# Cross-attention and tree-routed FFN on one core: both layer norms scaled by ScalarE, the constant score rows copied by DMA, and batch 2's score parts made between the first scores

## What is computed

```python
def layernorm(x): return (x - mean(x)) / sqrt(var(x) + 1e-5)      # over the features
# part 1: causal attention of 16 heads of 16, weights scaled so that scores are large
xn = layernorm(x)
q, k, v = xn @ w_q.T, ctx @ w_k.T, ctx @ w_v.T                    # split into 16 heads
x = x + softmax(causal(q k^T / 4)) v @ w_o.T
# part 2: three trees (q, k, v) of depth 4 route each token to one of 16 leaf MLPs (256 -> 64 -> 256)
z = layernorm(x)
q, k, v = fff_q(z), fff_k(z), fff_v(z)
x = x + softmax(q k^T / 16) v
```

## Time and profile before

| what | value |
|---|---|
| median of 3 runs | 679.64 us (678.51 to 679.95) |
| the profiled execution | 676.23 us |
| its span, first to last instruction | 674.4 us |
| around the span | 1.8 us |
| mean granted TensorE clock | 0.948 |
| PE busy | 558.6 us (83%) |
| DVE busy | 488.7 us (72%) |
| POOL busy | 355.2 us (53%) |
| ACT busy | 307.1 us (46%) |

### The profile page before, as it was taken

How to read it: one execution, slowest core, us unless ns; L and a number is a source line. 1 busy time by engine, 2 the same in 40 slices (tenths; PEclk the granted TensorE clock), 3 DMA queues, 4 the chain that set the end, 5 groups by cost and what they waited for, 6 DMA issues and landing times.

```text
span 674.4 us, 15294 instructions
## 1 busy us (share of the span) xinstructions
PE 558.6 (83%) x5375; PEld 454.7 (67%) x5375; DVE 488.7 (72%) x1411; ACT 307.1 (46%) x508; POOL 355.2 (53%) x452
## 2 busy tenths in 40 slices
PE   7637899989899888989888775849998888679996
PEld 6525678756676666767666553738887777569995
DVE  3887678999999999999998874772555455046664
ACT  3201555544454454445444452006876766433231
POOL 6551444466675675666656558512105666565642
PEclk9967999999999999899999997878999999999999
DMA  6696578757867875786776149847999999756663
GB/s 185 188 294 182 192 241 249 215 182 243 263 193 238 258 214 197 236 235 195 227 233 206 56 145 303 249 142 265 357 361 400 343 386 337 247 154 195 188 190 124
DMA packets 105715, 156.98 MB, mean 233 GB/s; under 512 B 12362, under 2 KB 75946, under 8 KB 105642
## 3 DMA queue, kind: packets, MB, share of 16 engines
q1 hardware_dynamic: 93786, 129.45, 60.7%
q0 software_dynamic: 9216, 25.18, 11.7%
q10 hardware_dynamic: 2640, 1.40, 0.7%
HBM read 84.20 MB, written 71.30 MB: 231 GB/s over the span
## 4 chain that ended last, share of the span: by engine, by line
PE 41%; DVE 27%; issue 13%; POOL 8%; ACT 5%; DMA 4%; another core or an unknown queue 1%; DVEq 0%; SPq 0%; POOLq 0%; ACTq 0%
DVE mneg L1194 8%; PE banks L841 5%; PE banks L527 5%; DVE xn L1142 4%; PE banks L830 4%; PE banks L902 4%; PE banks L856 4%; POOL xs_dram L1584 3%; PE banks L923 3%; DMA xb<-xs_dram 3%; POOL pt L1596 2%; PE banks L694 2%; PE banks L561 2%; ACT pt L956 2%; PE banks L891 2%
## 5 line engine op out<-in xcount | busy, mean ns | idle before, releaser
L956 ACT ACTIVATE pt<-banks 128x768 f32<-128x768 f32 x128 | 103.5, 811 | 102.4 <-PE banks L562 76.9
L1596 POOL TENSOR_SCALAR_AFFINE_SELECT pt<-pt 128x512 f32<-128x512 f32 x128 | 81.9, 641 | 123.0 <-ACT pt L956 120.5
L1194 DVE TENSOR_REDUCE mneg<-banks 128x6 f32<-128x768 f32 x128 | 121.0, 948 | 15.1 <-PE banks L536 10.5
L1584 POOL DMA_INDIRECT xs_dram<-xn2s,place x96 | 95.9, 999 | 53.8 <-issue 16.4
L534 PE MATMUL banks<-k,q 96*128 96x128 bf16 x256 | 52.3, 227 | 52.6 <-DVE mneg L1194 51.7
L534 PEld LDWEIGHTS banks<-k,q 96*128 96x128 bf16 x256 | 25.5, 100 | 69.7 <-DVE mneg L1194 40.8
L577 PE MATMUL banks<-pt,vp 128*32 128x256 f32 (+1 forms) x1024 | 57.2, 343 | 9.3 <-issue 6.2
L561 PE MATMUL banks<-q,k 98*128 98x256 bf16 x256 | 57.0, 276 | 1.6
L1677 POOL DMA_INDIRECT q_all<-ys_dram,place x32 | 31.2, 976 | 45.9 <-DMA ys_dram<-yb 27.9
L535 PE MATMUL banks<-k,q 124*128 124x128 bf16 x256 | 51.9, 225 | 0.0
L536 PE MATMUL banks<-k,q 124*128 124x128 bf16 x256 | 51.6, 223 | 0.0
(11 more groups left out here) (182 smaller groups left out, 1426.9 us busy)
## 6 DMA issues: line engine op xcount, KB each, us to landing
ys_dram<-yb SPq DMA_DIRECT2D x36, 512.0 KB
xb<-xs_dram SPq DMA_DIRECT2D x35, 512.0 KB
xs_dram<-zero SPq DMA_DIRECT2D x45, 256.0 KB
xs_dram<-zero SPq DMA_DIRECT2D x18, 384.0 KB, 4.7
parts_dram<-kp SPq DMA_DIRECT2D x16, 384.0 KB
k<-parts_dram SPq DMA_DIRECT2D x32, 192.0 KB
parts_dram<-qp SPq DMA_DIRECT2D x16, 384.0 KB
q<-parts_dram SPq DMA_DIRECT2D x32, 192.0 KB
```

The costliest lines, as they stand in the source:

```text
L956: nc.scalar.activation(pt[:, 2 * p:2 * p + 2, 0:S + P], st_banks(b, p)[:, :, 0:S + P], ACT.Exp, scale=SC / QS).then_inc(exp_sb, 1)
L1194: nc.vector.tensor_reduce(mneg[b % 2][:, 2 * j:2 * j + 2, :], two[:, :, 0:S + P].rearrange("p e (i k) -> p e i k", k=P), axis=AX.X, op=ALU ...
L1584: gp.indirect_dma_start(xs_dram[tree], bass.IndirectOffsetOnAxis(ap=place[:, k:k + 1], axis=0), xn2s[m % RING][:, t, :], None).then_inc(sc ...
L1596: pool.affine_select(out=diag, in_=diag, compare_op=ALU.is_ge, fill=0.0, base=0, pattern=[[0, 2 * T], [1, P]], channel_multiplier=-1).then ...
```

## The change

Both norms are scaled by ACT, as an activation `Identity` with `scale` = rs and `bias` = -mean times rs. POOL makes that bias with two more instructions of 128x2 per norm, so `rstd1` and `rstd2` count by two. In the loop ACT has the second norm at j == 3, ahead of `weighed(b, 0)` and of the second part of q, and the first norm at j == 6, ahead of the copy of the values. `kw` and `qw` are half as wide, both are built at the start of POOL's list, and POOL's four casts are gone: SP copies the rows of buffer 0 to buffers 1 and 2, with four DMAs behind the unloading of batch 1 and ahead of `load_x(3)`. DVE's cast of `q4[0]` moves to just behind the first statistics. In the ramp, the second parts are made by ACT. The projections, transposes and parts of batch 2, and the norm of batch 3, stand between the first natural scores on PE and between their maxima on DVE.

```diff
+            def const_copy(z):                                              # SP
+                sp.wait_ge(const_rows[0], 2)
+                for full in (q4, k4):
+                    sp.dma_start(full[z][KS:P, :, :], full[0][KS:P, :, :]).then_inc(const_rows[z], 16)
...
                 unload(1, 1)
                 unload(1, 0)
+                for z in range(1, BUFS):
+                    const_copy(z)
                 load_x(3)
...
-                pe.wait_ge(c_in[2], 16)                                     # PE, ramp
-                pe.wait_ge(k1_sb, 1)
-                pe.wait_ge(kr_sb, 1)
-                project(W_BANKS[0], wk, lambda c: ct[2][:, c, :]).then_inc(k_ps, 1)
...
-                transpose_in(2)
-                pe.wait_ge(xnT_sb, 3)
-                pe.wait_ge(v_sb, 1)
-                project(G7, wq, lambda c: xnT[:, c * S:c * S + S]).then_inc(q_ps, 1)
                 for j in range(PAIRS):
                     first_scores(j)
-                    if j == 5:
+                    if j == 1:
+                        transpose_in(2)
+                    if j == 2:
+                        pe.wait_ge(xnT_sb, 3)
+                        pe.wait_ge(v_sb, 1)
+                        project(G7, wq, lambda c: xnT[:, c * S:c * S + S]).then_inc(q_ps, 1)
+                    if j == 4:
+                        pe.wait_ge(c_in[2], 16)
+                        pe.wait_ge(k1_sb, 1)
+                        pe.wait_ge(kr_sb, 1)
+                        project(W_BANKS[0], wk, lambda c: ct[2][:, c, :]).then_inc(k_ps, 1)
+                    if j == 6:
                         transpose_in(3)
...
+            def norm_out(b):                                                # ACT
+                act.wait_ge(rstd1, 2 * (b + 1))
+                ge(act, xnT_ps, b - 1)
+                for t in range(T):
+                    nc.scalar.activation(xn[b % 2][:, t, :], xt[b % 2][:, t, :], ACT.Identity, scale=rs1[:, t:t + 1],
+                                         bias=mr1[:, t:t + 1]).then_inc(xn_done, 1)
+            def norm2_out(b, u):
+                act.wait_ge(rstd2, 2 * (b + 1))
+                ge(act, xn2T_ps, b - 1)
+                if b >= RING:
+                    for r in range(TREES):
+                        scattered(act, r, b - RING)
+                for t in range(T):
+                    nc.scalar.activation(xn2s[b % RING][:, t, :], x1[u][:, t, :], ACT.Identity, scale=rs2[:, t:t + 1],
+                                         bias=mr2[:, t:t + 1]).then_inc(xn2_sb, 1)
...
+                    if j == 3 and has(b, -2):
+                        norm2_out(b - 2, u)
                     if j == 3 and has(b, -1):
                         weighed(b, 0)
...
+                    if j == 6 and has(b, LEAD + 1):
+                        norm_out(b + LEAD + 1)
                     if j == 6 and has(b, 1):
...
+                norm_out(0)                                                 # ACT, ramp, behind the cast of k4[0]
                 first_part(kp, K1, W_BANKS[0], k_ps, 0, k1_sb, 1.0)
...
+                copy_xnT(0)
+                second_part(kp, K2, k_rem, kr_sb, 0, k2_sb)
+                q_parts(0)
+                norm_out(1)
+                k_parts(1, W_BANKS[1])
+                copy_xnT(1)
+                q_parts(1)
                 act.wait_ge(consts, 2)
                 act.wait_ge(v_ps, 1)
...
+                norm_out(2)
+                copy_xnT(2)
+                q_parts(2)
+                k_parts(2, W_BANKS[0])
+                norm_out(3)
...
-                    if j == 2 and has(b, -2):                               # DVE, loop
...
-                            nc.vector.tensor_scalar(xn2s[(b - 2) % RING][:, t, :], x1[u][:, t, :], mv2[:, t, 0:1],
-                                                    rs2[:, t:t + 1], ALU.subtract, ALU.mult).then_inc(xn2_sb, 1)
                     if j == 5 and has(b, -1):
                         divide(b, 1)
-                    if j == 5 and has(b, LEAD + 1):
-                        norm_out(b + LEAD + 1, u)
...
                 norm_in(0, 0, 0)                                            # DVE, ramp
+                v.wait_ge(q_factor, WIDE + 1)
+                nc.vector.tensor_copy(q4[0][KS:P, :, :].rearrange("p h (i k) -> p (h i) k", k=P),
+                                      qf.unsqueeze(1).to_broadcast([P - KS, NH * T, P])).then_inc(const_rows[0], 1)
                 k_parts(0, W_BANKS[0])
-                norm_out(0, 0)
                 norm_in(1, 0, 1)
-                norm_out(1, 1)
                 q_parts(0)
                 k_parts(1, W_BANKS[1])
+                q_parts(1)
                 norm_in(2, 1, 0)
...
                 for j in range(PAIRS):
                     first_maxima(j)
-                    if j == 1:
-                        norm_out(3, 1)
+                    if j == 3:
+                        q_parts(2)
+                    if j == 4:
+                        norm_in(3, 1, 1)
+                    if j == 5:
+                        k_parts(2, W_BANKS[0])
                 last_maxima(0)
...
                 pool.tensor_scalar(ve[:], mv[:, :, 1], EPS, None, ALU.add).then_inc(var_sem, 1)   # POOL, rsqrt
-                gp.wait_ge(var_sem, b + 1)
+                pool.tensor_scalar(mr[:], mv[:, :, 0], -1.0, None, ALU.mult).then_inc(var_sem, 1)
+                gp.wait_ge(var_sem, 2 * (b + 1))
                 pool.tensor_tensor(rs[:], ve[:], mhalf[:], ALU.pow).then_inc(rstd_sem, 1)
+                gp.wait_ge(rstd_sem, 2 * b + 1)
+                pool.tensor_tensor(mr[:], mr[:], rs[:], ALU.mult).then_inc(rstd_sem, 1)
...
-                for z in range(1, BUFS):                                    # POOL, ramp
-                    pool.tensor_copy(k4[z][KS:P, :, :], kf.unsqueeze(1).to_broadcast([P - KS, NH, S])
-                                     ).then_inc(const_rows[z], 1)
-                    pool.tensor_copy(q4[z][KS:P, :, :], qf.unsqueeze(1).to_broadcast([P - KS, NH, S])
-                                     ).then_inc(const_rows[z], 1)
...
+                for m in range(2, LEAD + 1):
+                    rsqrt(m, aggr1, mv1, ve1, var1, rs1, mr1, rstd1, (xn_done, m * T))
```

More of the change, by code:

```diff
@@ L161, in build @@
         mv1, mv2 = at("mv1", [P, T, 2]), at("mv2", [P, T, 2])
-        ve1, ve2, rs1, rs2 = (at(n, [P, T]) for n in ("ve1", "ve2", "rs1", "rs2"))
+        ve1, ve2, rs1, rs2, mr1, mr2 = (at(n, [P, T]) for n in ("ve1", "ve2", "rs1", "rs2", "mr1", "mr2"))
         mhalf = at("mhalf", [P, T])
@@ L542, in parts_in @@
                 if j == 0 and b < BUFS:
-                    pe.wait_ge(const_rows[b], 2)
+                    pe.wait_ge(const_rows[b], 32 if b else 2)
             def scores(b, n, u, j):
@@ L1135, in norm_in @@
                     nc.vector.bn_aggr(mv1[:, t, :], st1[:, t, :]).then_inc(aggr1, 1)
-            def norm_out(b, s):
-                v.wait_ge(rstd1, b + 1)
-                ge(v, xnT_ps, b - 1)
-                for t in range(T):
-                    nc.vector.tensor_scalar(xn[s][:, t, :], xt[s][:, t, :], mv1[:, t, 0:1], rs1[:, t:t + 1],
-                                            ALU.subtract, ALU.mult).then_inc(xn_done, 1)
             def divide(b, par):
@@ L1370, in allocate, with third_part, k_parts, q_parts @@
                     tt(owner[:], owner[:], inside1[:], ALU.add).then_inc(alloc, 1)
-            def all_parts(b, ps, part, slots, rem, first_sem, rem_sem, second_sem, third_sem, scale):
-                remainder(b, ps, part, slots[0], rem, first_sem, third_sem, rem_sem, scale)
-                v.wait_ge(rem_sem, b + 1)
-                nc.vector.tensor_copy(part[b % 2][:, slots[1], :], rem[:]).then_inc(second_sem, 1)
-                v.wait_ge(second_sem, b + 1)
-                nc.vector.tensor_tensor(part[b % 2][:, slots[2], :], rem[:], part[b % 2][:, slots[1], :],
-                                        ALU.subtract).then_inc(third_sem, 1)
+            def third_part(b, part, slot, second, rem, ready, done):
+                v.wait_ge(ready, b + 1)
+                nc.vector.tensor_tensor(part[b % 2][:, slot, :], rem[:], part[b % 2][:, second, :], ALU.subtract).then_inc(done, 1)
+            def k_parts(b, ps):
+                remainder(b, ps, kp, K1, k_rem, k1_sb, k3_sb, kr_sb, 1.0)
+                third_part(b, kp, K3, K2, k_rem, k2_sb, k3_sb)
+            def q_parts(b):
+                remainder(b, G7, qp, Q1, q_rem, q1_sb, q3_sb, qr_sb, QS)
+                third_part(b, qp, Q3, Q2, q_rem, q2_sb, q3_sb)
             def first_maxima(j):
@@ L1523, in _ @@
                                pattern=[[-1, P]], channel_multiplier=1).then_inc(ident_ok, 1)
-            def halves(ap):
-                return ap.rearrange("p (h j) -> p h j", h=T)
             def factors_k():
@@ L1564, in late_consts, with rsqrt @@
                 gp.wait_ge(b2_zero, 1)
-            def rsqrt(b, aggr, mv, ve, var_sem, rs, rstd_sem, prev_read):
```

(9 more changed lines are left out.)

72 lines of the change are left out of this document (21 added, 51 removed).

## The result

The changed kernel took **674.67 us** (median of 4 runs, 673.75 to 675.62) beside 679.8 for the kernel before: ratio 0.9928 [0.9908, 0.9947], 5.1 us gained where I had forecast 27 and a range that ended at 665. It is faster, by 2 to 5 us, which is under 1%.

A forecast was written before the change was run, and what follows sets the result against it. DVE was taken to set the step, with PE 3.1 us behind. Ramp 11.5 plus steps 16.4 less tail 1.0 gave 26.9 us off 676.23, so 649.3; with 3.4 for the median, 652.7 us, range 641 to 665.

The forecast's parts named there:

- Steps, 16.4: Steps: 16.4 us gained of 32.6 removed from DVE; 1.6 a step in steps 3 to 11, 1.0 in 13 and 14.
- steps above 23 us: Sign named beforehand: if full steps stay above 23 us, where 21.8 was forecast, the sum is wrong there.
- Bound by PE behind DVE: Full step of 23.40 us: DVE, busy 21.78, sets it; PE, 3.1 us behind, limits what comes back.
- Ramp, 11.5: Ramp: last maximum of batch 0 12.1 us earlier, at 44.2, less 0.6 for a late load: 11.5 us gained.
- the 0.6 of the text: Step 0: cost of the load of x(4) coming late behind SP's new DMAs, 0.6 us (0 to 4).
- The Trainium skill's rules: Two rules weighed: norms on ACT would lose in the steps; the moved cast could cost 2 us of ramp, giving 654.7.
- ACT: ACT's norms in the steps: 0.44 us a scaling, 0.9 a pair, 1.8 a step; bias about 0.5 behind rs.
- The ring of my slower rival: Steps, j == 3 and j == 6: ACT waits for POOL's bias, POOL for exponentials; 3.0 us a step, 713, chance 0.03.
- Tail, -1.0: Tail of the attention: 1.0 us lost, from an exponential in step 15 delayed 2.5 us behind a norm on ACT.
- The rivals: Five alternatives: PE or ACT limits, SP's queue, all DVE time back, slower, casts not the cause; chances 0.17, 0.13, 0.06, 0.03, 0.03.
- PE or ACT sets the step: Steps: each gives 0.4 us instead of 1.6, some 5.5 in all, time 663.6 us; chance 0.17.

The follow-up runs named there:

- e4: Changed kernel with POOL's third parts of q and k in the steps replaced by memsets (left out from batch 3 on): ratio 0.9866 to the kernel before.
- e12: Kernel before, norms still on DVE, with POOL's third parts of q and k in the steps as memsets: ratio 0.9922.
- e17: Changed kernel with POOL's third parts and causal selects in the steps as memsets, so it computes less: 652.66 us, ratio 0.9628.
- e18: Kernel before, norms on DVE, with POOL's third parts and causal selects in the steps as memsets: ratio 0.9861 to the kernel before.
- e3: Changed kernel's ramp, but from step 5 no engine scales a norm and nobody waits for a bias: 671.28 us, ratio 0.9911.
- e16: The changed kernel itself, measured again on another chip: 676.22 us beside 678.51 for the kernel before, ratio 0.9979.
- e15: Changed kernel with the last three second norms on DVE and the ramp's cast of `q4[0]` moved later: 674.33 us, ratio 0.9931.
- e8: Kernel before with its own ramp, and both norms of the steps on ACT with POOL's bias: ratio 1.0131.
- e1: Changed kernel's ramp, with both norms of the steps back on DVE: ratio 0.9933 to the kernel before.
- e11: Changed kernel with only the last three second norms (steps 15 to 17) back on DVE: 674.21 us, ratio 0.9937.
- e14: Changed kernel with k's third part in the steps on DVE and the last three second norms back on DVE: ratio 0.9945.
- e5: Changed kernel with third parts as memsets, and POOL's old subtraction for k run behind into an unread scratch tile: ratio 1.0081.

## Why the prediction was wrong, point by point

- **Steps, 16.4: the step that failed.** "What is taken from DVE comes back only as far as PE lets it" took 1.82 us of `xn` and 1.07 of `xn2s` as DVE's own time. A pair is 0.73 of its own; 1.1 and 0.3 were block, and the block stayed when the instruction went. Measured: 216.4 to 215.4 us over steps 3 to 11, 1.0 instead of 14.4; steps 13 and 14 gave 0.0 instead of 2.0. The prediction's own sign of this, steps above 23 us, came. I had seen the same thing in the ramp (the earlier trace rows beside the earlier trace rows) and priced it there; in the step the rows showed it too, and I gave the block away with the norm. e4, e12, e17 and e18 show this by taking POOL's reads away, with the rival named there. That the norms' own 1.5 us a step vanish as well while the blocks are in place is measured (e3); how they divide into longer small instructions and new short waits I read from the timelines alone. The sign of the forecast came out right by the ramp alone.
- **Bound by PE behind DVE**: right, and nearer than thought. Without blocks the plain step gains about 0.5, not 1.6; that PE's list then sets it is my reading.
- **Ramp, 11.5**: 10.3 at M0 (46.08, forecast 44.2), with the first score at 28.5 as forecast; but the same kernel has M0 at 47.80 in e16, so the gain is 8.6 to 10.3. Then step 0 took 20.61 instead of 17.60, 3.0 us that I had at 0.6; in e16 it took 18.49. So ramp and step 0 together gave 7.3 and 7.7 us, not 11.5. In the fifteen traces with the new ramp step 0 took 18.4 to 18.9 us in seven, and in these the granted clock was 1.00 from 55 to 65 us; in the other eight it took 19.97 to 20.9, and part of that stretch was at 0.65 or 0.66. e15 and e16, whose step 0 took 20.89 and 18.49:

```profile
60.00:65.00 5.00, 4.47 (x22) 3.28 (x20) 1.78 (x2) 2.87 (x5) 2.13 (x4) 0.66 0.85 223
```
```profile
60.00:65.00 5.00, 3.56 (x33) 3.00 (x34) 2.58 (x3) 3.63 (x6) 3.01 (x7) 1.00 1.01 229
```

  So some 2 of the 3.0 us go with the clock. About 1 is left, which may be the late stacks and loads, near the 0.6 of the text, or the clock again (its mean over step 0 was 0.90 before, 0.82 to 0.87 in the seven); no run separates them. Why the clock rises later in one execution than in another with the same ramp stays open.
- **The Trainium skill's rules.** The Trainium skill (SBUF — State Buffer, Who interferes with whom) was right where I weighed it: the moved cast held POOL's first instruction for 2.18 us, worth 1.1 at the first norm (e15). The same section of the Trainium skill says what I didn't use, that a DVE instruction with two SBUF inputs contends with a POOL instruction that reads SBUF but not with one that only writes. The traces agree: `moved` takes 1.21 us beside the subtraction and 0.21 in e4, beside nothing that reads. The Trainium skill's rule for such work, VectorE and not ScalarE (ScalarE: Activation LUTs, Rules for kernel authors), bears on the time per element, and the trace agrees: 1.09 us a pair on ACT, 0.73 on DVE where nothing blocks it. As a forecast of the time it was right behind the old ramp, 1.3% slower (e8), and not behind the new one, where e1 and the changed kernel are equal.
- **ACT.** 1.09 a pair for 0.9 (the median of one is 0.592; I had 0.44 by columns, from rows with other operands). The Trainium skill (ScalarE: Activation LUTs, What ACT_TABLE_LOAD costs) has the price: 186 ns + 0.833 a column, and 93 for each pointer operand, by which one instruction here is estimated at 0.585 us. The trace agrees with its 0.592; I should have set it beside my estimate. The bias came 0.6 us behind where rs would have been, for 0.5. The ring of my slower rival exists in small: waits of 0.97, 0.97 and 1.75. It decides in the drain.
- **Tail, -1.0**: -4.05, and e11, e14 and e15 put 2.9 to 3.4 of it down to the second norm on ACT in steps 15 to 17. I had let 1.0 of 2.5 us through in step 15; the whole delay (2.86) went on, and more behind it.
- **The rivals**: none had it. "PE or ACT sets the step" came nearest in size (663.6), for another reason.

## What to carry to other kernels

The time of a DVE instruction beside one of POOL may not be its own: if the two end together, price it at its unblocked time and ask which instruction stands there next. Before moving work off an engine, leave it out altogether once (e3): one run gives the ceiling. And weigh a step moved in a loop in the drain as well, where nothing covers it.

## What was unexpected of the hardware

- Memsets of POOL beside the same DVE instructions cost those with two inputs nothing (`moved` 0.21 in e4), but scalings with one input still waited for them: `inside` on 128x48 took 0.91 us in e17 and ended with a memset, where it takes 0.24 alone, and the pair of `xn` took 1.41 in e18, beside two memsets, where it takes 0.73 alone and 1.08 was expected.
- In single full steps the granted clock fell from 1.00 to between 0.88 and 0.93, and some of these steps were about 2 us longer (26.48 beside 24.13 in e5, 25.45 beside 23.44 in e8). The trace of the changed kernel has no such step, that of e16, the same kernel, has one at 0.87; what sets it off stays open.
- Copies of 32 rows within SBUF took SP 0.93 to 1.38 us of issue each, twice the 0.6 that I had taken from a load. The load of x right behind them took 1.28 as well, and 0.6 in the later steps, so it is this stretch and not the copy that makes an issue long.
